# Feed-forward with int8 activations: rounding in one addition, fp16 halves of fp32 words as TensorE's stationary operand

## The reference, cut to what matters

```python
def act_quant(x):
    scale = 127.0 / jnp.clip(jnp.max(jnp.abs(x), axis=-1, keepdims=True), 1e-05)
    return jnp.clip(jnp.round(x * scale), -128, 127) / scale
def weight_quant(w):
    scale = 1.0 / jnp.clip(jnp.mean(jnp.abs(w)), 1e-05)
    return jnp.clip(jnp.round(w * scale), -1, 1) / scale
def bit_linear(x, w): ...      # einsum('bsd,hd->bsh', act_quant(x), weight_quant(w))
h = bit_linear(x, w1)          # 512 -> 2048
h = depthwise_conv1d(h.transpose(0, 2, 1), conv_w, conv_b)   # three taps over tokens
h = jax.nn.silu(h.transpose(0, 2, 1))
return bit_linear(h, w2)       # 2048 -> 512
x = x + _L0_ffn_ref(_layernorm(x, axis=-1), ...)
```

## Time and profile before

| | us |
|---|---|
| median of 3 executions (lowest to highest) | 1976.48 (1971.2 to 1978.28) |
| the profiled execution, its own time | 1974.42 |
| its span, first to last instruction | 1972.6 |
| feed-forward, first left tap to last residual | 300.9 to 755.1 |

### The profile page before, as it was taken

How to read it: one execution, slowest core, us unless ns; L and a number is a source line. 1 busy time by engine, 2 the same in 40 slices (tenths; PEclk the granted TensorE clock), 3 DMA queues, 4 the chain that set the end, 5 groups by cost and what they waited for, 6 DMA issues and landing times. The chain is left out here.

```text
span 1972.6 us, 31643 instructions
## 1 busy us (share of the span) xinstructions
PE 1650.0 (84%) x8834; PEld 714.7 (36%) x8834; DVE 1320.0 (67%) x1895; ACT 1137.3 (58%) x1851; POOL 1086.3 (55%) x755
## 2 busy tenths in 40 slices
PE   4888717798988974789999999999999984799998
PEld 2444313343433422333333333333333321344443
DVE  5988777888887786466666675757665653655653
ACT  3444338787777863356565656565655552666563
POOL 3455504777777882246565656465665652554542
PEclk9888859999998996799999999999999987899999
DMA  8121000000000002111010111111010101010101
GB/s 304 55 74 53 0 1 0 1 1 1 0 0 1 0 1 96 59 31 54 25 53 24 51 30 48 32 32 48 27 52 23 39 5 64 1 43 21 43 21 43
DMA packets 60442, 72.00 MB, mean 36 GB/s; under 512 B 14416, under 2 KB 40016, under 8 KB 59856
## 3 DMA queue, kind: packets, MB, share of 16 engines
q1 hardware_dynamic: 57520, 62.62, 10.1%
q10 hardware_dynamic: 2848, 8.52, 1.1%
HBM read 37.40 MB, written 8.39 MB: 23 GB/s over the span
## 5 line engine op out<-in xcount | busy, mean ns | idle before, releaser
L1283 DVE TENSOR_REDUCE s_mx<-bank 128x1 f32<-128x512 f32 x512 | 334.0, 675 | 245.2 <-PE bank L1388 242.6
L1209 ACT ACTIVATE s_E<-bank 128x512 f32<-128x512 f32 x512 | 293.3, 594 | 225.2 <-PE bank L1402 195.3
L1133 POOL TENSOR_TENSOR s_E<-s_E 128x1024 f32<-128x1024 f32 x128 | 300.0, 2355 | 154.5 <-PE bank L1410 128.8
L587 POOL TENSOR_TENSOR f_y<-f_y,f_t 128x511 f32<-128x511 f32 x128 | 167.3, 1309 | 108.2 <-DVE f_y L767 101.5
L1388 PE MATMUL bank<-s_KA,s_QA 96*128 96x512 f16 x512 | 193.7, 389 | 24.0 <-DVE s_mx L1283 14.8
L1402 PE MATMUL bank<-s_QA,s_KA 97*128 97x512 f16 x512 | 197.8, 388 | 12.0 <-ACT s_E L1209 8.0
L1126 POOL TENSOR_TENSOR s_qkl<-s_qkf,s_qkh 128x512 f16<-128x512 f32 x64 | 74.1, 1157 | 192.7 <-ACT s_qkh L1187 192.7
L1566 POOL TENSOR_TENSOR m_xl<-m_xf,m_xh 128x512 f16<-128x512 f32 x64 | 91.2, 1434 | 109.5 <-ACT m_xh L1609 109.5
L915 PE MATMUL bank<-f_w2q,w2raw 128*128 128x512 bf16 x512 | 132.2, 402 | 9.9 <-DVE w2raw L882 7.1
L1410 PE MATMUL bank<-s_E,s_V 128*32 128x512 f32 x1024 | 137.9, 611 | 2.8 <-ACT s_E L1209 2.8
L1287 DVE RECIPROCAL bank<-bank 128x128 f32<-128x128 f32 x128 | 121.3, 952 | 24.5 <-PE bank L1418 24.5
(11 more groups left out here) (235 smaller groups left out, 4047.9 us busy)
## 6 DMA issues: line engine op xcount, KB each, us to landing
X<-in_x SPq DMA_DIRECT2D x8, 1024.0 KB, 7.1
s_QA<-s_qkh SPq DMA_DIRECT2D x256, 32.0 KB, 1.8
s_KA<-s_qkh SPq DMA_DIRECT2D x256, 32.0 KB, 1.8
out_x<-X SPq DMA_DIRECT2D x8, 1024.0 KB, 4.2
a_cf<-in_ctx SPq DMA_DIRECT2D x8, 768.0 KB, 4.8
s_cf<-in_ctx SPq DMA_DIRECT2D x8, 768.0 KB, 4.5
w1raw<-in_w ACTq DMA_DIRECT2D x1, 4096.0 KB, 14.0
w2raw<-in_w ACTq DMA_DIRECT2D x1, 4096.0 KB, 29.2
```

The source lines that it names most:

```text
L587: e.tensor_tensor(o, o, t[:, j % NTP, 0:S - 1], ALU.add).then_inc(s_c3.sem, 1)
L1133: e.tensor_tensor(into, into, other, ALU.add).then_inc(s_sum.sem, 1)
L1209: e.activation(E[:, SLOT[k] + h, :], SC[u % 2][:, :], ACT.Exp, scale=1.0 / float(np.sqrt(DH)))\
L1283: e.tensor_reduce(mx[:, q, h:h + 1], MX[q % 2][:, :], AX.X, ALU.max).then_inc(s_red.sem, 1)
```

## The change

`g` times `s2b` is no longer rounded by an addition and a subtraction. One addition of `RAISE` = 1.5 times 2 to the 23 plus 0x6600 leaves an fp32 word whose low 16 bits, read as fp16, are 1536 plus the rounded integer. TensorE reads those halves: `gq` now holds fp32 words, and the stationary operand is every second fp16 of them. The 1536 is taken off again by four matmuls of a constant -1536 with the column sums of `w2q`, which open each accumulation (`unshift`). The column sums are made once, by 16 matmuls in batch 0. `w2q` is fp16 in place of bf16.

Ranks move from VectorE to ScalarE, `BY_ACT` grows from 6 to 11; ScalarE's `raised` goes away. `zh` and `zl` of the odd batches get buffers of their own, `t` has 3 buffers for 4, and `part` has one buffer, shared with `diag`. `maxima` moves from step 5 to step 4, `high` from steps 10 to 13 to steps 10, 11, 11, 12, `low` to 11, 11, 12, 12, the last statistics from step 12 to 11.

```diff
-        w1q, w2q = sb("w1q", [P, KD * F], F16), sb("w2q", [P, KF * D], BF16)
+        w1q, w2q = sb("w1q", [P, KD * F], F16), sb("w2q", [P, KF * D], F16)
...
-        gq = w2raw[:, 0:NQ * S // 2].bitcast(BF16).rearrange("p (j s) -> p j s", s=S)
...
+        gq = w2raw[:, 0:NQ * S].rearrange("p (j s) -> p j s", s=S)
+        whole16 = w2raw[:, 0:NQ * S].bitcast(F16).rearrange("p (j s t) -> p j s t", s=S, t=2)
...
-        NY, NTP, GJ = 4, 4, 4
+        NY, NTP, GJ = 4, 3, 4
...
-        BY_ACT = (2, 5, 8, 11, 13, 14)
+        BY_ACT = (1, 2, 4, 5, 7, 8, 10, 11, 12, 13, 14)
+        SHIFT = 1536.0
+        RAISE = ROUND + 0x6600
...
             def late(b, odd, j):
-                s_c3.wait(e, b, j + 1 - NTP)
+                s_c3.wait(e, b, j + 1 - NTP if odd or j >= NTP else min(j - 1, 0))
...
-            def raised(b, odd, r):
-
+            def whole(b, odd, r):
+
+                slot(e, b, r)
                 s_u.wait(e, b, r + 1)
-                o = g(odd, ORDER[r])
-                e.activation(o, o, ACT.Identity, bias=round_c[:, 0:1]).then_inc(s_up.sem, 1)
-
-            def whole(b, odd, r):
-
-                slot(e, b, r)
-                s_up.wait(e, b, nact(r + 1))
-                e.activation(gq[:, r % NQ, :], g(odd, ORDER[r]), ACT.Identity, bias=nround[:, 0:1]).then_inc(s_ga.sem, 1)
+                e.activation(gq[:, r % NQ, :], g(odd, ORDER[r]), ACT.Identity, bias=shift[:, 0:1]).then_inc(s_ga.sem, 1)
...
-                    if ahead and 10 <= j < 10 + KD:
-                        high(b + 1, 1 - odd, j - 10, zbank(j - 10))
+                    if ahead:
+                        for c in in_step(lambda c: (10, 11, 11, 12)[c] if c < KD else -1, j):
+                            high(b + 1, 1 - odd, c, zbank(c))
...
-                e.tensor_scalar(gq[:, r % NQ, :], g(odd, ORDER[r]), ROUND, ROUND, ALU.add, ALU.subtract)\
-                    .then_inc(s_gq.sem, 1)
+                e.tensor_scalar(gq[:, r % NQ, :], g(odd, ORDER[r]), RAISE, None, ALU.add).then_inc(s_gq.sem, 1)
...
-                        for c in in_step(lambda c: (10, 11, 11, 12)[c] if c < KD else -1, j):
+                        for c in in_step(lambda c: (11, 11, 12, 12)[c] if c < KD else -1, j):
                             low(b + 1, 1 - odd, c, zbank(c))
...
+            def unshift():
+                for q in range(TT):
+                    e.matmul(OB[q][:, :], nshift[:, :], w2sum[:, :], start=True, stop=False)
...
-                    last = e.matmul(OB[q][:, :], gq[:, r % NQ, q * P:(q + 1) * P], w2q[:, ORDER[r] * D:(ORDER[r] + 1) * D],
-                                    start=(r == 0), stop=(r == KF - 1))
+                    last = e.matmul(OB[q][:, :], whole16[:, r % NQ, q * P:(q + 1) * P, 0], w2q[:, ORDER[r] * D:(ORDER[r] + 1) * D],
+                                    start=False, stop=(r == KF - 1))
...
+                    if not has_a and j == 3:
+                        e.wait_ge(s_wq, 2)
+                        for i in range(KF):
+                            last = e.matmul(AB[:, :], ident16[:, :], w2q[:, i * D:(i + 1) * D],
+                                            start=(i == 0), stop=(i == KF - 1))
+                        last.then_inc(s_ws, 1)
-                    if has_a and j == 5:
+                    if has_a and j == 4:
                         maxima(b - 1)
```

More of the change, by code:

```diff
@@ L510, in ternary_ffn @@
         wsum, wm, wr = sb("wsum", [P, 2]), sb("wm", [P, 2]), sb("wr", [P, 2])
-        nround, round_c = sb("nround", [P, 1]), sb("round", [P, 1])
+        nround, round_c, shift = sb("nround", [P, 1]), sb("round", [P, 1]), sb("shift", [P, 1])
+        ident16, nshift, w2sum = sb("ident16", [P, P], F16), sb("nshift", [P, P], F16), sb("w2sum", [P, D], F16)
         HB, AB, OB = banks[0:3], banks[3], banks[4:8]
@@ L581, in scaled, with tap @@
                 e.tensor_tensor(o, o, s2b[:, :], ALU.mult).then_inc(s_u.sem, 1)
-            def tap(b, j):
+            def tap(b, odd, j):
                 s_t.wait(e, b, j + 1)
@@ L586, in tap @@
                 o = y[:, j % NY, 0:S - 1]
-                e.tensor_tensor(o, o, t[:, j % NTP, 0:S - 1], ALU.add).then_inc(s_c3.sem, 1)
+                e.tensor_tensor(o, o, t[:, (j + odd) % NTP, 0:S - 1], ALU.add).then_inc(s_c3.sem, 1)
             def step(b, odd, has_a, has_c, ahead, ahead2):
@@ L598, in step @@
                         ln_p(e, b + 2)
-                    tap(b, j)
+                    tap(b, odd, j)
             ln_p(e, 0)
@@ L669, in step @@
                         mine += [(b - 1, 1 - odd, r) for r in in_step(act_step, j) if on_act(r)]
-                    for m in mine:
-                        raised(*m)
                     middle(b, odd, j)
@@ L681, in step @@
                         spread_out(b - 1)
+                    if not has_a and j == 6:
+                        e.wait_ge(s_ws, 2)
+                        e.activation(w2sum[:, :], AB[:, :], ACT.Copy).then_inc(s_wq, 1)
                     if ahead and j in (4, 5):
@@ L704, in _ @@
             silu(B - 1, 1, KF - 1, True)
-            for r in (11, 13, 14):
-                raised(B - 2, 0, r)
+            for r in (10, 11, 12, 13, 14):
                 whole(B - 2, 0, r)
@@ L775, in largest @@
                     s_pk.wait(e, b, 0)
+                elif k == 1:
+                    s_bc.wait(e, b, 0)
+                else:
+                    s_pk.wait(e, b, 2 * k - 1)
                 src = others if odd and k < NG // GJ else pairs
-                e.tensor_reduce(part[:, k % 2, :] if k else top[:, :],
+                e.tensor_reduce(flat if k else top[:, :],
                                 src[:, GJ // 2 * k:GJ // 2 * (k + 1), :, :].rearrange("p j s i -> p s j i"),
@@ L781, in largest @@
                     s_pk.wait(e, b, 2 * k)
-                    e.tensor_tensor(top[:, :], top[:, :], part[:, k % 2, :], ALU.max).then_inc(s_pk.sem, 1)
+                    e.tensor_tensor(top[:, :], top[:, :], flat, ALU.max).then_inc(s_pk.sem, 1)
             def scales(b):
@@ L792, in scales @@
                 s_am2.wait(e, b, 3)
+                s_pk.wait(e, b, s_pk.per)
                 s_bc.wait(e, b, 0)
@@ L864, in _ @@
             steps(e, step)
-            for r in (10, 12):
-                whole(B - 2, 0, r)
             largest(B - 1, 1, 3)
@@ L924, in linear2, with transposed @@
                         s_zl.wait(e, b + 2, KD)
+                    unshift()
                 rounded(e, b, r)
                 products(r)
-            def transposed(b, c, has_c):
+            def transposed(b, c, has_c, first):
                 if c == 0:
                     s_r2.wait(e, b, TT)
+                    if first:
+                        e.wait_ge(s_wq, 3)
                     s_s2b.wait(e, b - 1, 0)
@@ L950, in step @@
                         for c in in_step(lambda c: (10, 11, 12, 12)[c] if c < KD else -1, j):
-                            transposed(b + 1, c, has_c)
+                            transposed(b + 1, c, has_c, not has_a)
             e.wait_ge(s_ws, 1)
```

39 lines of the change are left out of this document (20 added, 19 removed).

## The result

| | before | after |
|---|---|---|
| median of 4 executions, us (lowest to highest) | 1977.38 (1971.2 to 1980.25) | 1953.67 (1950.91 to 1955.98) |
| the profiled execution, its own time | 1974.42 | 1954.25 |
| its span | 1972.6 | 1952.4 |
| feed-forward, first left tap to last residual | 454.2 | 434.2 |
| all that stands behind the feed-forward | 1217.5 | 1218.0 |

The ratio of the times is 0.9878, with a 95% interval of 0.9853 to 0.9903: 23.7 us faster, where 40.4 were forecast. In the profiled executions the whole difference of 20 us lies in the feed-forward.

A forecast was written before the change was run, and what follows sets the result against it. VectorE's in-order list with two bubbles was taken as the bound: 56.0 - 2.6 - 3.5 - 2.5 = 47.4, plus 1.6, gave 49.0 us a steady batch. All batches and the tail summed to 40.4 us less: 1936 us, range 1922 to 1963.

The forecast's parts named there:

- the first rival: Whole feed-forward: half the gain is given back, a steady batch takes 53 us, 1959 us in all; chance 0.19.
- VectorE's list with two bubbles: Steady batch: VectorE's in-order work, 47.9 us busy plus 7.1 us of waits, bounds the 56.0 us.
- The five roundings a batch: VectorE, steady batch: five of ten roundings leave its list, 2.6 us off; the five that stay cost 0 more.
- What takes over: Steady batch: 1.6 us added, between 0 and 6, for uneven queues and VectorE sharing with GpSimd, giving 49.0 us.
- 43.75 of 49 us, 89%: GpSimd, steady batch: keeps its 34 instructions and 43.75 us of work in a batch of 49 us.
- 3.57 us bubble: VectorE's wait for transposed maxima before L786: read as 3.6 us, 3.5 to come off with `maxima` in step 4.
- the 3.5 before `low`: VectorE's wait for ScalarE's `high`, in two pieces: 2.5 us to come off, 1.0 us of wait kept.
- Half of it is given back: GpSimd, ScalarE and VectorE hold each other up: steady batch 53 us, 1959 us in all; chance 0.19.
- VectorE and GpSimd shutting each other out: 13 VectorE instructions each wait out a whole GpSimd one: 13.1 us more, batch 60.5 us, 2003 us; chance 0.04.
- The strided read: TensorE reading every second fp16 slows the second matmuls to 0.43 us: batch 59.1 us, near 2011 us; chance 0.04.
- Batch 0: First feed-forward batch: 16 column-sum matmuls put 3.4 us on TensorE, part caught up, so +1.0 us.
- The tail: After the last batch: two roundings leave VectorE's list, GpSimd's last product and TensorE's matmuls set most; 1.0 us less.

The follow-up runs named there:

- b_moves: The kernel before with only the four moves (transposes of the maxima, `high`, `low`, last statistics): 1964.6 us, ratio 0.9933, steady batch 53.1 us.
- a_act13: The kernel after with ranks 3 and 6 also rounded by ScalarE, not VectorE: 1956.3 us, ratio 0.9876, steady batch 52.2 us.
- a_half_products: The kernel after with GpSimd multiplying only half of each row, the rest left unscaled: 1944.6 us in one run, steady batch 49.6 us.
- a_scales4: The kernel after with VectorE's scales moved from step 3 to step 4: 1954.3 us, ratio 0.988, steady batch 52.0 us.
- a_max5: The kernel after with the transposes of the maxima back in step 5: 1967.6 us, ratio 0.9942, steady batch 54.4 us.
- a_copies_back: The kernel after with `high`, `low` and the last statistics in their old steps: 1965.0 us, ratio 0.9925, steady batch 53.1 us.
- a_no_moves: The kernel after with all four moves undone, keeping the new rounding, ranks and buffers: 1974.9 us, ratio 0.9985, steady batch 54.9 us.
- a_contig: The kernel after with 128 adjacent fp16 as the second matmul's stationary operand: 1964.6 us in one run, steady batch 52.3 us.
- a_no_shift: The kernel after without the four `unshift` matmuls and 15 of 16 column-sum matmuls: 1961.6 us in one run, steady batch 52.3 us.

## Why the prediction was right and wrong

**What held.** The sign held, and 1953.7 lies in the range of 1922 to 1963. The size did not: 23.7 us of the 40.4 came. The range was drawn wide enough to take in the first rival, and the number fell in by that width, not by the sum. A steady batch, at 52.3, left the 47 to 51 us of the forecast and stayed just under the 53 at which the prediction called itself wrong. VectorE's list with two bubbles was the right thing to read in the waits, and taking the bubbles away gave most of what was gained (b_moves, 18.3 of 20.0 us). The five roundings a batch and `raised` gone came as written, no idle stood before L789 in batch 3, and before `low` there was none where about 1 us was expected. Undisturbed, a rounding with fp32 output takes 0.41 us as with bf16, so the 0 put in for that was right. The clock read 0.97 and 1.00 in the two steady batches shown, as taken. Batch 6 came near (-4.3 for -4.4), and batch 7 less so (-2.3 for -3.3): there 2.5 of the 4.5 us before the maximum of the transposes stayed.

**The step that failed** is the 1.6 us in "What takes over", put in for the unevenness between the queues and for the sharing of VectorE and GpSimd. It measured 4.9: 52.3 less the 47.4 of the list. Two things were wrong in it.

*First, the load of GpSimd was read as a mean over the batch.* "43.75 of 49 us, 89%" leaves 5 us of room. By the half of the batch there was little: 30.2 of 32.7 us in steps 7 to 15 already before. With that load the half could shrink by 2.5 us at most, and shrank by 1.6. The forecast had taken three roundings (2.1 us) and a bubble of 2.5 from the very half. The row needed was a window cut inside the batch. a_act13 bears this out: 3 us less of VectorE there changed its length by 0.1. A second limit lies close behind, though, for with half of the products gone the half still takes 29.0.

*Second, the clash.* VectorE's list measured 49.95 us where it was to be 45.3, and a_half_products, with the same list beside a lighter GpSimd, 44.8. The prediction looked at 13 instructions, four normalisations, four rescalings and five roundings, and left most of them at the lengths already seen; they hold 2.5 of the 4.7 us. The other 2.2 lie in instructions that it did not name, `largest` (0.6) and L792 with L799 (1.6). It missed that the chain behind the transposes, which had stood in the lee of the bubble with GpSimd idle, would now run beside GpSimd's products. L792 at 1.33 us for 0.17 is the row for that in batch 3 (the diagonals in batches 2 and 4). The cause is shown three times: the lengthened instructions end at a fixed distance behind the end of a GpSimd instruction, L792 follows the length of the product (a_half_products), and the lengths come back where GpSimd waits (a_scales4). So of the 3.57 us bubble 2.1 were gained (a_max5), and of the 3.5 before `low` 0.8 (a_copies_back). The roundings, "2.6 us", gave 1.1 with all that came with them (a_no_moves), for those that stayed grew from 3.6 to 4.7 us together there, and to 5.1 in the kernel after.

Smaller errors of the sum did not decide it. TensorE, put at 45.3 us, was busy 46.2 and 47.7 in the two steady batches shown. The "0.44 us for four" transposes are the distance of their starts; the row itself reads 0.60.

**The rivals.** *Half of it is given back* described the result best: 53 us a batch and 1959 in all, for 52.3 and 1953.7, nearer than the forecast's 49.0 and 1936. It had a chance of 0.19. Its wording, that GpSimd and VectorE hold each other up, is what the halves show. ScalarE is no part of it, for it was busy 40 to 44 us and took two more roundings without a longer batch.

*VectorE and GpSimd shutting each other out*: the mechanism is real and its price was too high, 4.7 us a batch for 13.1. The mark set for it was a mean above 1.1 us of L748 and L759. L748 stayed at 0.98, as before, and L759 rose from 0.77 to 1.17 for the four of batch 3 that read `w1raw`, so one of the two passed the mark. Which forms are hit can be read: additions and multiplications from SBUF to SBUF, down to 128x4 numbers, and sums of two SBUF operands (L785), but not the taps and `low`, which read one operand from PSUM, nor the large reductions. The Trainium skill, "SBUF — State Buffer", section "SBUF: two separate sides", names these kinds, a two-port mode or two inputs in SBUF, and the rows agree. What is waited out is what is left of GpSimd's instruction: all of it for L792 in batch 3, which started together with a product, and little where the two meet late. The rival had charged the whole of one, and its own length on top, each time.

*The strided read* is refuted by a_contig: 104 ns against 104.

**Batch 0**: +2.1 for +1.0. I had put down that part of the 3.4 us of the column sums would be caught up. Nearly all of them were paid (about 3 us, by a_no_shift and the means above); spreading the matmuls avoids most of it (40.6 and 40.7).

**The tail**: +1.9 for -1.0. TensorE is busy 27.9 us for 25.9 at a clock of 0.83 for 0.87, with four more matmuls. Whether the slower clock or a later product of the last ranks makes it was not settled.

**Left open**: what binds the 29 us of steps 7 to 15 once GpSimd is lighter, and what lowers the clock in the part behind the feed-forward, which takes up to 13 us more in one execution than in another.

## What to carry to other kernels

When several engines are near the same load, cut the period at the places where their loads change before reading how much room is left: an engine at 78% of a batch may be at 92% of the half in which the gain is to fall. A bubble is worth less than its length where the work behind it ran undisturbed because of it; look at who will run beside that work once it starts earlier. And an edit of 4 us in one part of a long program is judged by that part's own length when the rest moves by 10 us from one execution to the next.
